# Reordering the units of an attention and router stage, and starting the first expert by halves

## What is computed

```python
h = concat([tokens(x), txt])                              # (32, 69, 256)
h = h + attn(layernorm(h), ...)                           # 16 heads of 64
h = h + ffn(layernorm(h), w_g, c_fc, c_proj)              # 8 experts, top 2
# attn, per head:
scores = q @ k.T / sqrt(64);  attn = softmax(scores, axis=2)   # over the queries
out = (attn @ v).reshape(B, S, 1024) @ l_w.T + l_b
# ffn:
logits = xt @ w_g;  top_v, top_i = top_k(logits, 2);  probs = softmax of the two
rank = cumsum(one_hot(top_i)) - 1; dropped where rank >= cap (690)
h = gelu(exp_batches @ c_fc);  exp_out = h @ c_proj       # 690 rows per expert
out = sum over the two experts of probs * exp_out
```

## Time and profile before

| | us |
|---|---|
| median of three runs | 730.72 |
| the three runs | 726.61, 730.72, 731.09 |
| the profiled execution | 728.92 |
| its span, first to last instruction | 727.2 |
| TensorE busy | 693.2 (95%) |
| VectorE busy | 506.7 (70%) |
| ScalarE busy | 291.5 (40%) |
| GpSimd busy | 281.3 (39%) |

### The profile page before, as it was taken

One profiled execution on the slowest core, in us unless ns is written; L12 is line 12 of the kernel. 1 busy time (PEld: TensorE's weight loads), 2 busy tenths in 40 slices (PEclk: granted clock), 3 DMA queues, 4 the chain that ended last, 5 costly groups with the idle time before them and its releaser, 6 DMA issues.

```text
span 727.2 us, 16884 instructions
## 1 busy us (share of the span) xinstructions
PE 693.2 (95%) x6651; PEld 653.0 (90%) x6651; DVE 506.7 (70%) x1143; ACT 291.5 (40%) x652; POOL 281.3 (39%) x294
## 2 busy tenths in 40 slices
PE   8699999999999999999999886999999999999995
PEld 6588899899898998989989886999999999999995
DVE  6687887878978789787877571747575665647471
ACT  4354544544444454444544221514343332425130
POOL 4564010030401304012030345365666666666706
PEclk9989999999999999999999897999999999999998
DMA  9651000000000000000000413343434535444202
GB/s 265 172 160 31 1 2 17 3 17 17 19 16 2 18 18 18 17 2 18 17 18 18 131 35 98 90 89 98 92 86 91 125 73 136 101 92 101 21 10 29
DMA packets 51521, 42.99 MB, mean 59 GB/s; under 512 B 25435, under 2 KB 45081, under 8 KB 51457
## 3 DMA queue, kind: packets, MB, share of 16 engines
q1 hardware_dynamic: 22289, 30.49, 13.8%
q0 software_dynamic: 29168, 11.61, 10.0%
HBM read 32.76 MB, written 10.25 MB: 59 GB/s over the span
## 4 chain that ended last, share of the span: by engine, by line
PE 67%; DVE 18%; issue 4%; SPq 4%; ACT 3%; DMA 2%; POOL 1%; POOLq 0%; DVEq 0%; ACTq 0%
PE pair L1420 11%; PE pair L1422 11%; PE pair L1421 11%; PE lone L1420 8%; PE lone L1421 7%; PE lone L1422 7%; PE pair L1538 3%; PE ct_ps L1548 3%; DVE zsum L1063 3%; DVE vals L1073 2%; DVE top L1054 2%; PE vt_ps L1525 2%; DVE expo L1057 2%; SPq L456 2%; ACT expo L826 1%
## 5 line engine op out<-in xcount | busy, mean ns | idle before, releaser
L768 POOL DMA_INDIRECT out<-yrow,held x48 | 100.9, 2102 | 74.7 <-DVE yrow L1382 60.6
L949 ACT ACTIVATE act_f<-pair 128x348 f32<-128x348 f32 (+1 forms) x128 | 51.8, 457 | 97.8 <-PE pair L1422 97.8
L1420 PE MATMUL pair<-xe_hi,fc_hi 128*128 128x348 f32 (+1 forms) x256 | 82.9, 324 | 1.1 <-DVE xe_lo L1363 1.1
L1422 PE MATMUL pair<-xe_hi,fc_lo 128*128 128x348 f32 (+1 forms) x256 | 83.2, 325 | 0.0
L1421 PE MATMUL pair<-xe_lo,fc_hi 128*128 128x348 f32 (+1 forms) x256 | 83.2, 325 | 0.0
L751 POOL DMA_INDIRECT held<-token_rows,found_ix x48 | 69.2, 1442 | 28.8 <-issue 21.9
L1420 PE MATMUL lone<-pj_hi,act_hi 128*116 128x256 f32 (+1 forms) x256 | 72.1, 282 | 0.0
L1422 PE MATMUL lone<-pj_hi,act_lo 128*116 128x256 f32 (+1 forms) x256 | 71.9, 281 | 0.0
L1421 PE MATMUL lone<-pj_lo,act_hi 128*116 128x256 f32 (+1 forms) x256 | 71.8, 280 | 0.0
L812 ACT ACTIVATE qkv<-lone,bq_sb 128x276 f32<-128x276 f32 x100 | 48.6, 486 | 55.8 <-PE lone L1422 55.8
L812 ACT ACTIVATE qkv<-pair,bq_sb 128x276 f32<-128x276 f32 x92 | 44.7, 486 | 55.0 <-PE pair L1422 55.0
(11 more groups left out here) (246 smaller groups left out, 1991.1 us busy)
## 6 DMA issues: line engine op xcount, KB each, us to landing
raw_fc<-c_fc SPq DMA_DIRECT2D x8, 1024.0 KB, 7.0
raw_pj<-c_proj SPq DMA_DIRECT2D x8, 1024.0 KB, 7.4
raw<-w_qkv SPq DMA_DIRECT2D x6, 512.0 KB, 7.6
raw<-patches SPq DMA_DIRECT2D x6, 384.0 KB, 4.9
out<-h SPq DMA_DIRECT2D x8, 276.0 KB
token_rows<-sent POOLq DMA_DIRECT2D x7, 285.7 KB, 7.2
qkv<-patches SPq DMA_DIRECT2D x3, 384.0 KB, 10.0
raw<-w_l SPq DMA_DIRECT2D x1, 1024.0 KB, 7.7
```

The costliest lines, as they stand in the source:

```text
L768: pool.indirect_dma_start(out, bass.IndirectOffsetOnAxis(ap=xg[p][0:n, t, D:D + 1].bitcast(U32), axis=0), yrow[p][0:n, t, :], None, bounds ...
L949: gelu = act.activation(act_f[f % 2][:, a:b], pair[f % 2][:, h, 0:b - a], ACT.Gelu)
L1420: pe.matmul(dst, l_hi, r_hi, start=(first and n == 0), stop=False)
L1422: done = pe.matmul(dst, l_lo, r_hi, start=False, stop=(last and n == len(terms) - 1))
```

## The change

The parts, all in one program:
- On TensorE the value transposes of a unit stand ahead of the contexts of the unit before, in all 64 units.
- The chain of the group before moves forward: projection halves in units 0 and 1 (before 0 and 2), transposes of y, residual and statistics in unit 2 (3), rows to send in 3 (4), their transposes in 4 (5), logits and picks in 5 (6), the count at the end of unit 6, behind its blocks (before in unit 7 ahead of them), the place in unit 7 as before, now for the last group's predecessor too. The Exp of the gap is in unit 6 (7). The order of bank uses follows.
- Last group: heads 0 to 2 of its projection in unit 62, 3 to 5 in unit 63, 6 behind the last context, 7 behind six fillers. The table of group 6 and four fillers now stand ahead of the transposes of y, not behind the logits.
- Expert 0: the rows of the first half are turned (turn_first) and multiplied (expand_first, with first_gelu and first_act) for all eight blocks before the rows of the second half are multiplied; the second half is turned after the first four (EARLY) of them. Its place in stage_d then holds only the second half. The other experts are as before.

The diff, cut to what is spoken of (put_place is split in two functions, put_place and put_row, that run one behind the other):

```diff
     for m in range(ALL):
         order += unit_uses(m)
-    order += [("proj", last, c) for c in range(KD)] + [("ytr", last, n) for n in range(2)]
-    order += [("logit", last, 0), ("table", last - 1, 0), ("rank", last, 0), ("table", last, 0)]
+    order += [("table", last - 1, 0), ("ytr", last, 0), ("ytr", last, 1), ("logit", last, 0), ("rank", last, 0),
+              ("table", last, 0)]
...
     uses = []
     if g >= 1:
-        uses += {5: [("x2t", g - 1, c) for c in range(KD)], 6: [("logit", g - 1, 0)], 7: [("rank", g - 1, 0)]}.get(u, [])
+        uses += {4: [("x2t", g - 1, c) for c in range(KD)], 5: [("logit", g - 1, 0)]}.get(u, [])
+    if m == ALL - 2:
+        uses += [("proj", g, c) for c in range(KD)]
     uses += blocks[:2]
-    if g >= 1 and u == 3:
+    if g >= 1 and u == 2:
         uses += [("ytr", g - 1, n) for n in range(2)]
     uses += blocks[2:]
-    if g >= 1 and u in (0, 2):
-        uses += [("proj", g - 1, u // 2)]
+    if g >= 1 and u == 6:
+        uses += [("rank", g - 1, 0)]
+    if g >= 1 and u in (0, 1):
+        uses += [("proj", g - 1, u)]
...
                 if m >= 1:
                     put_ctx(Step((m - 1) // UNITS), (m - 1) % UNITS)
-                if g >= 1 and u in (1, 3):
-                    put_y(Step(g), -1, range(u // 2, u // 2 + 1))
+                if g >= 1 and u in (1, 2):
+                    put_y(Step(g), -1, range(u - 1, u))
                 if g + 1 < GROUPS and u == 5:
                     put_xT(Step(g), 1)
-                if g >= 1 and u == 5:
+                if g >= 1 and u == 4:
...
-                if g >= 1 and u == 7:
+                if g >= 1 and u == 6:
...
+            def put_first(h):
+                a, b = HALVES[h]
+                for c in range(KD):
+                    act.wait_ge(s_xe, KD * h + c + 1)
+                    act.activation(xe_hi[:, c, a:b], (vt_ps, ct_ps)[c][:, 0:b - a], ACT.Copy).then_inc(s_xe_hi, 1)
+            def first_gelu(f):
+                a, b = HALVES[0]
+                act.wait_ge(s_half_mid, f + 1)
+                if f >= 2:
+                    act.wait_ge(s_half_lo, f - 1)
+                act.activation(act_f[f % 2][:, a:b], pair[f % 2][:, 0, 0:b - a], ACT.Gelu).then_inc(s_half_gelu, 1)
+            put_first(0)
+            for f in range(EARLY):
+                first_gelu(f)
...
+                first = st.i == 0 and st.k is None
                 for f in range(KF):
                     wait(act, s_mid, st, lambda i: KF * i + f + 1)
                     wait(act, s_act_lo, st, lambda i: KF * i + f - 1)
-                    for h, (a, b) in enumerate(HALVES):
+                    if first and f < 2:
+                        act.wait_ge(s_half_lo, KF - 1 + f)
+                    for h, (a, b) in list(enumerate(HALVES))[first:]:
                         gelu = act.activation(act_f[f % 2][:, a:b], pair[f % 2][:, h, 0:b - a], ACT.Gelu)
...
-                if u == 3 and before:
+                if u == 2 and before:
                     residual(st, -1)
                     norm_mid(st, -1)
-                if u == 4 and before:
+                if u == 3 and before:
                     norm_mid_end(st, -1)
-                if u == 6 and before:
+                if u == 5 and before:
                     put_logits(st, -1)
                     pick(st, -1, 0)
                     pick(st, -1, 1)
-                if u == 7 and before and more:
+                if u == 7 and before:
                     put_place(st, -1)
+                    put_row(st, -1)
             for m in range(ALL):
                 unit(m)
             last = Step(GROUPS)
             low_ctx(Step(GROUPS - 1), UNITS - 1)
...
-            put_place(last, -2)
+            add_table(last, -2)
             norm_last()
             put_logits(last, -1)
             pick(last, -1, 0)
             pick(last, -1, 1)
             norm_mid_end(last, -1)
-            add_table(last, -2)
             share_last()
             put_place(last, -1)
+            put_row(last, -1)
...
+            low_first(0)
             dve.wait_ge(s_h2_out, 16 * GROUPS)
+            for f in range(EARLY):
+                first_act(f)
...
                 more, before, blocks = g + 1 < GROUPS, g >= 1, m + LEAD < ALL
+                turn_values(m)
                 if m >= 1:
                     context(Step((m - 1) // UNITS), (m - 1) % UNITS)
-                turn_values(m)
                 if m + 1 < ALL:
                     score(m + 1)
+                if u == 4 and before:
+                    turn_x2(st, -1)
                 if u == 5 and before:
-                    turn_x2(st, -1)
-                if u == 6 and before:
                     logit(st, -1, "x2t", x2T, wg_sb)
-                if u == 7 and before:
-                    count(st, -1)
+                if m == ALL - 2:
+                    project_last(range(3))
+                if m == ALL - 1:
+                    project_last(range(3, 6))
                 if blocks:
                     project_qkv(m + LEAD, 0)
                     project_qkv(m + LEAD, 1)
-                if u == 3 and before:
+                if u == 2 and before:
                     turn_y(st, -1)
                 if blocks:
                     project_qkv(m + LEAD, 2)
-                if u in (0, 2) and before:
-                    project_out(g - 1, u // 2)
+                if u == 6 and before:
+                    count(st, -1)
+                if u in (0, 1) and before:
+                    project_out(g - 1, u)
                 if u == 1 and g >= 2:
                     tabulate(st, -2)
                 if u == 1 and g == 0:
@@ -1706,15 +1772,15 @@
             for m in range(ALL):
                 unit(m)
             last = Step(GROUPS)
-            project_last(range(4))
             context(Step(GROUPS - 1), UNITS - 1)
-            project_last(range(4, UNITS - 1))
-            project_last(range(UNITS - 1, UNITS))
+            project_last(range(UNITS - 2, UNITS - 1))
             pe.wait_ge(s_sub, ALL)
             spare(6)
+            project_last(range(UNITS - 1, UNITS))
+            tabulate(last, -2)
+            spare(4)
             turn_y(last, -1)
             logit(last, -1, "proj", yT, wg_mid)
-            tabulate(last, -2)
             spare(20)
...
+            def turn_first(h):
+                pe.wait_ge(s_xg[0][h], 16 * XT // 2)
+                for c in range(KD):
+                    if h:
+                        pe.wait_ge(s_xe_lo, c + 1)
+                    for t in range(XT // 2):
+                        m = SIZES[3 * h + t]
+                        done = pe.transpose((vt_ps, ct_ps)[c][:, t * XR:t * XR + m],
+                                            xg[0][0:m, 3 * h + t, c * 128:(c + 1) * 128], ident[0:m, 0:m])
+                    done.then_inc(s_xe, 1)
...
+            def expand_first(f):
+                if f >= 2:
+                    pe.wait_ge(s_half_gelu, f - 1)
+                expand(f, 0).then_inc(s_half_mid, 1)
+            turn_first(0)
+            pe.wait_ge(s_xe_lo, KD)
+            pe.wait_ge(s_fc_lo, 4)
+            for f in range(EARLY):
+                expand_first(f)
...
+                first = st.i == 0 and st.k is None
                 wait(pe, s_xe_lo, st, lambda i: 2 * KD * (i + 1))
                 wait(pe, s_fc_lo, st, lambda i: 4 * (i + 1))
                 for f in range(KF):
                     wait(pe, s_gelu, st, lambda i: KF * i + f - 1)
                     if f == 0:
                         wait(pe, s_yrow, st, lambda i: XT * i - 2)
-                    w = slice(f * 128, (f + 1) * 128)
-                    for h, (a, b) in enumerate(HALVES):
-                        done = three(pair[f % 2][:, h, 0:b - a],
-                                     [(fc_hi[:, k, w], fc_lo[:, k, w], xe_hi[:, k, a:b], xe_lo[:, k, a:b]) for k in range(KD)])
+                    for h in range(first, 2):
+                        done = expand(f, h)
```

More of the change, by code:

```diff
@@ L59 @@
 BANKS = 4
+EARLY = 4
 LEAD = 2
@@ L389, in program @@
             sem(n) for n in ("s_reach", "s_in_row", "s_spread", "s_blank", "s_parts"))
+        s_half_mid, s_half_gelu, s_half_hi, s_half_lo = (sem(n) for n in ("s_half_mid", "s_half_gelu", "s_half_hi", "s_half_lo"))
         s_part_of, s_wg_mid, s_last, s_denom, s_share = (sem(n) for n in ("s_part_of", "s_wg_mid", "s_last", "s_denom", "s_share"))
@@ L941, in _ @@
                 split_fc(Step(0), 0, q)
-            put_xe(Step(0), 0)
+            def put_first(h):
[12 more added lines that the diff above has]
+                first_gelu(f)
+            put_first(1)
+            for f in range(EARLY, KF):
+                first_gelu(f)
             def stage_d(st):
+                first = st.i == 0 and st.k is None
                 for f in range(KF):
@@ L1217, in put_place, with put_row, before @@
                                   begins[:, :].unsqueeze(1).broadcast_to(every_choice), ALU.is_ge).then_inc(s_reach, 1)
+            def put_row(st, shift):
```

(53 more changed lines are left out.)

4 lines of the change are left out of this document (2 added, 2 removed).

## The result

| | before | changed |
|---|---|---|
| median of seven runs each, us | 729.19 | 721.86 |
| the runs, us | 726.61 to 731.09 | 720.37 to 724.47 |
| ratio (95% interval) | | 0.9904 (0.9886 to 0.9921) |
| profiled execution, its span, us | 728.92, 727.2 | 720.37, 718.6 |

What follows compares the result with a forecast made beforehand. TensorE was taken as the bound, with hardly any idle time in steady groups and most left in the hand-over to expert 0. Terms: -0.4-0.6-1.6+0.5-4.4 = -6.5 us, from median 730.72 to 724; range 718.5 to 729.

Steps and rivals of the forecast that it cites:

- Part 1: All 64 units on TensorE: value transposes ahead of contexts save 0.15 us per unit, from 4.36 to 4.21.
- 8 x 0.15: Per group: the new order's saving over eight units, 1.2 us, set against stalls of 2.0 instead of 1.0.
- Part 2: Groups 1 to 6, chain a unit forward: with the order's saving, -0.1 us per group, -0.6 in all.
- crowd of unit 5: VectorE in unit 5: x's low parts and the picks hold unit 6's score 0.25 us and unit 7's 1.3.
- Part 3: Last group and tail: -1.6 us from earlier Exp and earlier transposes of y, +0.5 for a possible clock fall.
- Part 4: Expert 0 by halves: first expansion 5.55 us sooner, less 0.65 for turning and 0.5 stall, net -4.4 us.
- the same five low microseconds: Expert 0: about 5.1 us at low clock assumed again behind the earlier start; 2 us more gained if avoided.
- A: Whole kernel: the forecast itself, only the hand-over gains; chance 0.47.
- B: Unit order saves 0.25 per unit or expert 0's clock stays up: 3 or 2 us more, 719 to 721; chance 0.22.
- C: Groups: the unit order saves nothing and stalls win, +2.7+1.2 us, leaving 728; chance 0.22.
- D: VectorE's crowd in unit 5 delays groups over 1.1 us beyond the forecast 2.0: slower, 731 to 735 us; chance 0.05.
- E: Expert 0 and tail: VectorE holds back expansions (4 us, not 0.5), table waits longer: 728 to 730 us; chance 0.04.

Runs made afterwards that it cites:

- the filled kernel: Changed kernel with 18 spare matmuls ahead of the table, in TensorE's idle 2.06 us, and nothing else: 721.95 us, ratio 0.9891.
- both moves and the contexts first: Changed kernel with x's second half a unit earlier, group 6's table behind the logits, and contexts again ahead of value transposes: 714.81 us, ratio 0.9811.

## Why the prediction was right, and where only its total was

**Part 1.** The 0.15 per unit was right: 4.36 to 4.22 with the order alone. Contexts to score are 0.64 us apart, just as contexts to value transposes were, so the step that had no row costs a change like the others, and the bounds of 0 and 0.25 are out. The Trainium skill (TensorEngine Tiling (Array Packing), Tiling Modes) says that a change of tiling mode drains the engine, and gives no time for it. Read as in the prediction, with contexts and scores in different modes, it gives 0.15 too, and the trace agrees with its 0.64. What failed is what the "8 x 0.15" was taken for, a gain of the order on top of stalls that the chain makes. With the transposes first a group of the changed kernel has about 1.8 us of stalls, with the contexts first 0.7 (a group of 45.0 us, less 9.44 us of work of the group before and of x, less eight plain units of 4.22 or 4.36). So the order brings 1.1 us of stalls for the 1.1 it saves: the contexts delay ScalarE's copies of x, these the low parts, zsum and the picks, and the transposes of unit 7 pay. Told by units, it gains 0.68 in five of them and returns 0.68 in unit 6. In group 0 the same happens, and the forecast's 0.4 came out as 0.1.

**Part 2.** The crowd of unit 5 was right in kind and in size: zsum at 3.21 (said 3.2), picks 2.75 (2.75), 0.24 at the score held in unit 6 (0.25), and ahead of unit 7 and at its score 1.03 and 0.24 us more between starts than without a hold, 1.3 together (1.3). Of the two stalls of 0.20 and 0.25 in unit 4 the first isn't there, since zsum of unit 3 stood 6.78 behind unit 2's start where I had counted 7.0, and the rows to send hold their transposes for 0.13. A stall of 0.17 that I hadn't forecast is in unit 0 (7.44 us, but 7.28 in group 5, where the slow unit 7 ahead of it had let VectorE catch up): on VectorE the place of the tokens stands ahead of zsum and of the last context's low part, and the output projection waits for that. I had called the place covered. So stalls are 1.8 a group for my 2.0, and the order saves 1.1 for my 1.2: a group came out 0.30 shorter, against my 0.1 after rounding (0.2 before it). Group 1 gave 0.5, five usual groups would have given 1.5. Then the clock took 1.3 us back in group 4, and the six groups gave 0.70 for the forecast's 0.6. This agreement is partly chance.

**Part 3.** The chain to the transposes of y was right: 10.15 after the Exp (said 10.75; 11.87 before), the Exp 0.75 earlier (said 0.5), the table the last to be waited for (2.06 us idle, said some 3). That gives 0.75 + 1.72 = 2.5 us where I took 1.6. The term that was mis-sized is the clock: it fell, and it cost 1.5 us, not half of 1.0. Transposes and logits alone took 1.45 us more (3.03 for 1.58 in the filled kernel), and I had left out the twenty fillers behind them, which at half clock last 4.26 instead of 2.62 us and then themselves hold the counts: the choices are ready 1.1 us before these. Net -2.5 + 1.6 = -0.9, for -1.1, two errors that cancel.

**Part 4.** First expansion 2.05 after the first turn (said 2.0), stalls of the second pass 0.8 (0.5). From the first multiply to the end all twelve profiled executions take 258.9 to 259.1 us, so nothing of this part is lost or won behind it. The gain was 6.4 us in the changed kernel and 4.8 in the halves alone; I said 4.4, and 2 more if the clock doesn't fall. Both cases occurred: of the eight profiled kernels with halves three had no low clock in expert 0 and five had 3.4 us of it, and first turn to end is 277.7 in the former and 279.1 to 279.4 in the latter. The four without halves had 6.8 or 10.2 us, and 283.0 to 284.2. So "the same five low microseconds" is the term that was mis-sized: they were 0 or 3.4. I kept them because rows of before had them, and no term of the sum asked what the earlier start does to them; these 2.0 us are nearly the whole difference between -6.5 and the profiled -8.6. That execution is the fastest of the seven; the medians differ by 7.3. When the clock falls in expert 0 stays open: the same instructions ran with and without it. Expert 1's fetch began 4.6 us later, counted from the first turn, and held nobody.

**The rivals.** A is what came. By its own line at 723.4 the result, 721.9, counts as faster, just so: the interval (0.9886 to 0.9921) has one per cent inside it. B's clock (2 us more if the fall in expert 0 is avoided) happened in the profiled execution; B's larger saving of the order did not. C, no saving in part 1, is what the order comes to in this kernel, but by another way than it named: five units are shorter and unit 6 is longer by the wait behind it, and no group got longer than before except where the clock fell. D's mechanism is there at 1.3 us a group and stays below the point from which it decides. E's stalls in the second pass were 0.8 us, not 4.

**What the order costs here.** Steady groups are equal with either order, and yet the contexts first are 1.6 us (with halves; the intervals overlap) and 2.9 us (without; they don't) faster. The profiles show two places. In the four executions with transposes first and the wait of 0.93, unit 7 ran at half clock in six of 24 groups, 1.3 us net each; in the five kernels where that wait is shorter or gone, no unit 7 in 30 groups did (one slow unit 5 apart). And in the tail TensorE idles 2.0 to 2.1 ahead of the table in the three kernels with transposes first and the table in front, and the clock is already low at the transposes of y; with the contexts first it idles 1.65, and transposes and table still run at full clock (in one of the two profiles the clock falls 1.0 us behind the start of the transposes, in the other not at all). That these two make up the whole difference of the medians is not shown.

## What to carry to other kernels

When a chain on a side engine is moved, write down that engine's own order for the unit it moves into, and look at which late input (here x) meets which long block (here the picks); moving one of the two by a unit gained more (0.68 us a group) than the whole reordering (0.30). Two edits that each save time on the busy engine don't add when both push the same side engine: measure them alone and together. And price a wait by what stands behind it too: two microseconds of idle time ahead of a serial stretch cost 3.8.

## What was not expected of the hardware

- The granted clock fell to half behind a wait of only 0.93 us, in some groups and not in others with the same instructions, and in the tail behind 2.06 us. The wait doesn't decide it alone: with both moves and the contexts first the clock fell once in unit 5 of group 1 (7.08 us for 5.56), where TensorE had not idled for more than 0.15 us at a time since the group began. In the profiles each slow stretch in groups, tail and expert 0 is 3.4, 6.8 or 10.2 us long. The spread of the runs follows them: the changed kernel with contexts first took 721.7 us in the two executions with a mean clock of 0.983, and 717.9 and 718.8 in the two with 0.990.
- Eighteen matmuls that compute nothing, put into the idle 2.06 us, brought the first turn of expert 0 forward by 1.5 us.
